# An attention and expert block: GpSimd's modulations of the third sequence wait for VectorE's row of maxima, routing and its table stand later

## The reference

```
h = layernorm(x) * (1 + ca) + sa
x = x + ga * attention(h)              # 16 heads of 16, causal, 1024 tokens
h = layernorm(x) * (1 + cb) + sb       # the modulations of this case
x = x + gb * experts(h)                # router: top 2 of 8, weights by softmax
                                       # expert: silu(h @ w1[e]) @ w2[e], 256 -> 512 -> 256
```

## Time and profile before

| | |
|---|---|
| median of 3 runs | 1007.19 us |
| lowest and highest | 1004.25 and 1008.59 us |
| the profiled execution | 1001.66 us, span 999.9 us |
| busy, share of the span | TensorE 90%, VectorE 72%, ScalarE 58%, GpSimd 37% |
| mean granted clock | 0.973 of full speed |

### The profile page before, as it was taken

The page is one execution under the profiler, slowest core; times in us unless marked ns, Lnnn a source line. Parts: engine busy times, 40 slices in busy tenths (PEclk is TensorE's granted clock), DMA queues, the critical chain, the costliest instruction groups (busy, mean ns, idle before and its releaser), DMA issues.

```text
span 999.9 us, 19445 instructions
## 1 busy us (share of the span) xinstructions
PE 899.6 (90%) x6174; PEld 531.4 (53%) x6174; DVE 719.7 (72%) x2314; ACT 581.7 (58%) x1271; POOL 367.0 (37%) x320
## 2 busy tenths in 40 slices
PE   5898899998999999889999997868899999999990
PEld 3543335433444443453543452523599899999980
DVE  8688766879657789857588769798638584444588
ACT  3335485776576677676666757667534533334563
POOL 1332021242324113345013453036387366555630
PEclk7899899999999999999999999999999999999996
DMA  8446447336324366250652746205413223222699
GB/s 282 127 65 129 57 86 142 60 44 143 61 40 111 56 119 135 74 77 15 132 92 93 164 70 195 78 26 152 113 58 122 95 70 106 75 77 72 193 298 320
DMA packets 83236, 110.62 MB, mean 111 GB/s; under 512 B 15930, under 2 KB 56434, under 8 KB 83138
## 3 DMA queue, kind: packets, MB, share of 16 engines
q1 hardware_dynamic: 75506, 89.45, 38.4%
q0 software_dynamic: 6816, 18.62, 6.0%
q10 hardware_dynamic: 816, 1.32, 0.4%
HBM read 69.42 MB, written 35.41 MB: 105 GB/s over the span
## 4 chain that ended last, share of the span: by engine, by line
PE 64%; DVE 12%; ACT 9%; issue 5%; DMA 5%; POOL 3%; SPq 2%; ACTq 0%; POOLq 0%; DVEq 0%
PE PO L1643 10%; PE PY L1520 10%; PE PH L1520 9%; PE PS L1623 8%; PE PM L1600 7%; ACT PR L1011 4%; PE PHT L1728 3%; PE PX L1655 2%; PE PX L1569 2%; DVE MXF L1324 2%; DVE JK L1321 2%; PE PS L1627 2%; PE PX L1578 2%; PE PX L1579 1%; DMA LD<-OS 1%
## 5 line engine op out<-in xcount | busy, mean ns | idle before, releaser
L1011 ACT ACTIVATE PR<-PS 128x512 f32<-128x512 f32 (+3 forms) x768 | 334.3, 497 | 147.0 <-PE PS L1627 112.4
L1321 DVE CUSTOM_DVE_ANT_0 JK<-PM,MK 128x128 bf16<-128x128 f32 (+3 forms) x512 | 239.5, 484 | 57.7 <-PE PM L1600 56.5
L1600 PE MATMUL PM<-QK 128*128 128x512 bf16 (+3 forms) x768 | 249.3, 333 | 23.6 <-DVE MXF L1324 14.2
L1623 PE MATMUL PS<-QK 128*128 128x512 bf16 (+3 forms) x768 | 247.2, 333 | 15.1 <-ACT PR L1011 11.0
L1324 DVE TENSOR_REDUCE MXF<-PM 128x1 f32<-128x512 f32 x256 | 175.2, 684 | 78.7 <-PE PM L1600 77.0
L1623 PEld LDWEIGHTS PS<-QK 128*128 128x128 bf16 x768 | 75.1, 98 | 174.5 <-ACT PR L1011 110.9
L1643 PE MATMUL PO<-PR,V 128*17 128x512 f32 (+3 forms) x1536 | 161.2, 492 | 0.0
L1600 PEld LDWEIGHTS PM<-QK 128*128 128x128 bf16 x768 | 75.6, 99 | 98.0 <-DVE MXF L1324 35.8
L1520 PE MATMUL PY<-W2S,HT 128*128 x852 | 118.9, 289 | 2.7 <-issue 1.8
L1520 PE MATMUL PH<-W1S,XT 128*128 x426 | 111.8, 398 | 0.9 <-DVE W2S L1474 0.9
L1627 PE MATMUL PS<-MT,identb 128*128 128x128 bf16 x512 | 112.1, 221 | 0.0
(11 more groups left out here) (269 smaller groups left out, 1206.1 us busy)
## 6 DMA issues: line engine op xcount, KB each, us to landing
QK<-SD SPq DMA_DIRECT2D x180, 128.0 KB
SD<-SP SPq DMA_DIRECT2D x42, 256.0 KB, 2.8
OP<-OS SPq DMA_DIRECT2D x64, 64.0 KB
LP<-LR SPq DMA_DIRECT2D x64, 64.0 KB, 2.4
W1S<-in_w SPq DMA_DIRECT2D x8, 512.0 KB, 5.5
X<-XA SPq DMA_DIRECT2D x3, 1024.0 KB, 8.0
H2D<-XA SPq DMA_DIRECT2D x3, 1024.0 KB, 4.9
YG<-YT SPq DMA_DIRECT2D x12, 256.0 KB, 4.7
```

Source lines behind the costliest of these rows:

```text
L1011: eng.activation(PR[:, slot, i, c0:512], PS[m % 3][:, c0:512], ACT.Exp, scale=0.25).then_inc(S["exp"].sem, 1)
L1321: eng.tensor_tensor_reduce(JK[:, jk % 2, 0:w], PM[m % 3][:, 0:w], MK[:, 512 - w:512], 1.0, -3.0e38, ALU.add, ALU.max, MXA[:, mb, h, qt:qt ...
L1600: eng.matmul(PM[m % 3][:, 0:128 * (k1 - k0)], QK[:, r, h, 0, qt * 128:(qt + 1) * 128], QK[:, r, h, 1, k0 * 128:k1 * 128], start=True, stop ...
L1623: last = eng.matmul(PS[m % 3][:, c0:512], QK[:, r, h, 1, j * 128:(j + 1) * 128], QK[:, r, h, 0, 512 * f + c0:512 * f + 512], start=True, s ...
```

## The change

Four numbers and one wait. The logits of sequence 2 stand two places later (18, 20, 22 of window 13 and place 0 of window 14, where they stood at 16 to 22). Routing's pieces stand two places later, the rounds of the table one. And GpSimd, ahead of the first modulation of sequence 2, waits for the sixth operation of group 14's chain. The lengths of all steps stay the same, and no instruction is added or taken away, except for the wait.

```diff
     for tp in range(4):
-        place(NG - 3, 16 + 2 * tp, logits(B - 2, tp))
-    place(NG - 2, 0, route(0, 1))
+        place(NG - 3, 18 + 2 * tp, logits(B - 2, tp))
+    place(NG - 2, 2, route(0, 1))
     place(NG - 1, 16, one("weights", 0))
-    for k, parts in table(0, 12, 0.5, 2):
+    for k, parts in table(0, 13, 0.5, 2):
         place(NG - 2, k, parts)
...
                     po.wait_ge(*after("h2a", *step))
+
+                    if b == B - 2:
+                        po.wait_ge(*after("cp", "cmax", NG - 2, 2, 5))
                     turn("h2")
```

## The result

The changed kernel takes 1013.78 us (median of 7 runs, 1010.71 to 1016.51), the kernel before 1006.76 us (7 runs beside them, 1004.25 to 1010.19): ratio 1.0064, 95% interval 1.0048 to 1.008. It is slower by 7.0 us. The profiled execution spans 1014.8 us with a mean granted clock of 0.967; it belongs to a run of 1016.51 us, the longest of the seven, while the one shown of before took 1001.66 us, less than any of its seven. So the two profiles lie 14.9 us apart, more than twice what the medians do, and a difference of spans must not be read as the cost of the change.

A forecast was written before the change was run, and what follows sets the result against it. VectorE was taken to limit group 14's second half, with VectorE and TensorE both near full in the first. 5.0 + 1.4 - 0.8 + 1.5 = +7.1 us on the median 1007.2 gave 1014.3 us, range 1009.2 to 1018.2.

The forecast's parts named there:

- The gate: Late modulations hold sequence 2's store on SP, then the row's store and load: group 14's first score +5.0 us (+4.2 to +7.2).
- TensorE idles 6: Ahead of group 14's first score, TensorE was to idle 6 us waiting for the row's load.
- The bytes ahead of the row: On SP's queue, the row's store needs its own 4.39 us; independent transfers would make the term 0.5 us smaller.
- Moved logits: At group 14's first score, logit work moved two steps later is still to do: +1.4 us (0 to +1.6).
- Table: One-hot rounds one step later shorten TensorE's waits at 666.33 and 671.37: -0.8 us (-2.5 to +0.5).
- Clock: Behind TensorE's stall, about 4.6 us of work at half clock: +1.5 us (0 to +3).
- (a): Rival: the stall is partly repaid as later waits shrink, about +2.5 us, 1009.7; chance 0.17.
- (c): Rival: VectorE counts through this stretch, its 4.7 us arrive whole with 0.8 from the table, 1001.7; chance 0.06.
- (b): Rival: the worse end, slower row store and load and a long spell at 1.2 GHz, +10.5 us, 1017.7; chance 0.11.
- (d): Rival: no effect, GpSimd's new wait is already met, 1007; chance 0.04.

The follow-up runs named there:

- e5: Kernel before plus one wait: SP holds sequence 2's store until a maximum of group 15 is read; 1010.05 against 1003.26 us, ratio 1.0075.
- e1: Changed kernel with the table's rounds back at their old place; 1013.13 against 1006.74 us, ratio 1.0074.
- e3: Changed kernel with SP's 1 MB store of sequence 2 placed behind group 14's row; 1002.61 against 1003.26 us, ratio 0.9995.
- e9: Changed kernel, row's store still held for the modulations but issued ahead of sequence 2's store, which goes behind the row's load; 1007.84 against 1002.60 us, ratio 1.005.
- e4: Kernel before with SP's store of sequence 2 placed behind group 14's row; 1007.47 against 1006.74 us, ratio 1.0002.
- e2: Changed kernel without GpSimd's wait, so the moves alone; 1003.11 against 1003.26 us, ratio 0.9999.
- e8: Kernel before with only the table's rounds one place later; 1007.56 against 1006.74 us, ratio 1.0009.
- e6: Changed kernel with 26 unread matmuls filling TensorE's stall ahead of its wait for the row; 1013.27 against 1006.74 us, ratio 1.0075.
- e7: Changed kernel with only the last four of the eight modulations waiting for the chain; 1003.12 against 1003.26 us, ratio 1.0014.

## Why the prediction came out

It said +7.1 us and 1014.3; the medians say +7.0 and 1013.78. The terms can be measured one at a time between neighbours of the table: 5.85 (first score, changed against before), 1.57 (behind the score, e5 against before: same order of work, clock lost), 0.62 (e1 against e5: logits and routing moved), -0.89 (changed against e1: table). They add up to 7.15, but they can't do otherwise: each is the step from one row of the table to the next, from before to changed.

- **The gate, +5.0: measured +5.85, and it is the cause.** e5 makes the whole loss with it alone, e3 takes the whole loss away. The chain's end was put 1.6 us earlier and came 1.3 earlier. The modulations took 10.89 us, H2D to load 5.30 us where sequence 0's analog had given 5.29, and load to score 2.93 us where I took 2.4; the row of such a wait had 2.80 and would have been the better choice. With the modulations ending 0.3 us later behind the second step than I had put them, that is nearly all of the missing 0.85. "TensorE idles 6" was 6.37.
- **The bytes ahead of the row: a side remark of mine failed.** I wrote that CD alone needs 4.39 us and that independent transfers would save 0.5 us. The 4.39 us of the earlier trace rows were themselves measured behind H2D; with nothing ahead the store lands in 1.45 us (e3, e9) or 3.06 (e4), so the order of the two stores is worth 3.4 us between e9 and the changed kernel, and at least 1.2 by the furthest pair of traces. The Trainium skill (DMA: Bandwidth & Descriptors, Queues, rings and completion order) has one ring's descriptors consumed in order; 1.45 against 4.87 us agrees with that; e4's 3.06 with nothing ahead isn't explained by it.
- **Moved logits, +1.4: measured +0.6 behind the score, and nothing without a stall.** In e2 the first score is 0.49 us earlier because less stands ahead of it, and with the table's 0.49 taken out the rest is 0.45 us longer behind it: a move, not a cost. I counted only what came behind. The 0.6 is from two single traces whose second stretches of half clock lie in different places, so it is rough.
- **Table, -0.8: measured -0.89, or -0.49 by the cleaner pair (e8).** The two waits shrank, 1.48 to 1.38 and 1.87 to 1.31 us.
- **Clock, +1.5: measured +1.57 (e5) and 1.31 (e6) in the traces, unproven by run times.** The half clock after the stall lasted 2.7 us (645.0 to 647.7), not 4.6, but all of it was full of matmuls on the critical path. A second stretch, which I hadn't foreseen, adds nothing in the changed kernel; in e5 the way up to group 15's row is 1.27 us longer than before and the rest, where the second stretch lies, 0.30. The Trainium skill (TensorE: Matmul & The Clock Gate, Why this matters for your kernels) warns of the fall after an idle gap, and the traces of the four kernels with 3.5 to 6.4 us of stall agree; e9's trace shows a fall behind 1.36 us as well.
- **Rivals.** (a) repayment falls: the way behind the score grew by 1.3 us, it didn't shrink. (c) falls by e3: with the row in time and all modulations waiting, VectorE's relief is worth 0.2 us. (b) falls with the gate at 5.85. (d) falls by GpSimd's [24.47 <-DVE CP L1348].

The mechanism came out, and the sum hit partly by luck: the gate was 0.85 too small and the logits 0.8 too large, and the half clock was shorter than I had put it and cost more per microsecond. No version tried is faster than the kernel before by more than the measurement can tell.

## What to carry to other kernels

When a step is delayed on an engine, look for what stands behind it in the program of another engine that takes its steps in order: here eight modulations held a store, the store held an unrelated small row, and the row held TensorE. The cure for such a gate is one line in the queue's order (e3), but first ask what the delay was to buy: slow steps on a busy engine are worth only what their consumer would use, and its next wait (here GpSimd's tiles) stands close behind. In e7, where fewer tiles came late, 1.3 us of the relief did reach TensorE. And measure a small transfer's latency where nothing is ahead of it before you call it its own.

## What the runs showed that I had not expected

- A 24 KB store landed 1.45 us after its issue alone in two traces and 3.06 in a third (e4), and 4.3 to 5.0 us after it in the six traces with a 1024 KB store issued 0.4 us ahead on the same queue. What made the 3.06 stays open.
- The granted clock isn't decided by the length of the last idle gap alone: behind 1.28 us of idle time it stayed at 1.00 (e7), behind 1.36 us the two windows from 638 to 642 show 0.60 and 0.55 (e9), in the same place of the program. e9's trace also shows 0.50 from 618 to 620 us, 3 to 5 us behind the chain's second step, where the changed kernel's trace shows 1.00 for the same order of work. And in the four kernels with a stall of 3.5 us or more a second stretch of some 3.4 us at half clock follows 30 to 36 us behind the first score; e4 has one without any stall. What decides it stays open.
- Behind the end of attention, where all twelve kernels do nearly the same work, their traces differ by up to 6 us (293.7 to 300.0), almost the size of the effect studied.
